# A retention and FP4-linear block on one core: v projected token-major, four heads at once, from group two on

## The reference

```python
xn = layernorm(x)
# retention, 16 heads of 64, on xn
q = heads((xn @ Wq + bq) * 64**-0.5); k = heads(xn @ Wk + bk); v = heads(xn @ Wv + bv)
ret = einsum('bhid,bhjd->bhij', q, k) * D        # D[i,j] = exp(decay_h * (i-j)) where i >= j, else 0
ret = ret / clip(abs(ret.sum(-1)), 1, None)
g = groupnorm_per_head(einsum('bhij,bhjd->bhid', ret, v)) * gn_w + gn_b
attn = (silu(xn @ Wg + bg) * g) @ Wo + bo
# linear layer whose input xn and weight are rounded to 4-bit values with block scales
lin = fp4(xn) @ fp4(weight).T * scale + bias
out = x + attn + lin
```

## Time and profile before

| | us |
|---|---|
| median of 3 runs | 2141.93 |
| lowest, highest | 2136.59, 2142.75 |
| the profiled execution | 2142.48 |
| its span, first to last instruction | 2140.7 |

### The profile page before, as it was taken

The page is one execution under the profiler, slowest core; times in us unless marked ns, Lnnn a source line. Parts: engine busy times, 40 slices in busy tenths (PEclk is TensorE's granted clock), DMA queues, the critical chain, the costliest instruction groups (busy, mean ns, idle before and its releaser), DMA issues.

```text
span 2140.7 us, 51098 instructions
## 1 busy us (share of the span) xinstructions
PE 2080.3 (97%) x18098; PEld 1053.5 (49%) x18098; DVE 1541.7 (72%) x4375; ACT 685.9 (32%) x1318; POOL 640.0 (30%) x456
## 2 busy tenths in 40 slices
PE   5988899999999999999999999999999999999999
PEld 3444444455455454555555555454555454555444
DVE  7899898988889877566767556767656767656732
ACT  5756623332223233322323322323322322322300
POOL 1323232332233333223332223233223233223220
PEclk8999999999999999999999999999999999999999
DMA  8878634334343443323333323333323333223343
GB/s 317 282 253 265 218 98 138 108 109 136 100 127 108 137 128 94 102 83 109 124 103 93 103 84 109 122 103 94 103 85 107 122 103 95 103 86 106 122 153 117
DMA packets 181686, 275.61 MB, mean 129 GB/s; under 512 B 117344, under 2 KB 117472, under 8 KB 181344
## 3 DMA queue, kind: packets, MB, share of 16 engines
q1 hardware_dynamic: 181600, 274.48, 39.8%
HBM read 204.18 MB, written 40.89 MB: 114 GB/s over the span
## 4 chain that ended last, share of the span: by engine, by line
PE 86%; DVE 11%; DMA 2%; issue 1%; ACT 0%; SPq 0%; DVEq 0%; ACTq 0%
PE mm L1288 54%; PE mm L1223 10%; PE tp L1223 6%; PE mm L1232 4%; PE tp L1298 3%; PE four L1338 3%; PE four L1351 2%; PE tp L1326 1%; PE four L1311 1%; PE four L1232 1%; PE tp L1251 1%; DVE wo L929 1%; DMA res<-in_w_f 1%; DMA parts<-wo 1%; DVE state L1041 1%
## 5 line engine op out<-in xcount | busy, mean ns | idle before, releaser
L1288 PE MATMUL mm<-xnT,wring 128*128 128x512 f16 x6144 | 1365.8, 381 | 13.8 <-DVE wring L929 6.8
L1288 PEld LDWEIGHTS mm<-xnT,wring 128*128 128x128 f16 x6144 | 598.2, 98 | 710.3 <-issue 25.2
L695 ACT ACTIVATE work<-four,gs 128x64 f32<-128x64 f32 x512 | 158.1, 414 | 554.2 <-DVE gs L1068 554.2
L556 POOL TENSOR_TENSOR yT<-gn,gate 128x512 f32 (+1 forms) x64 | 84.2, 1315 | 800.6 <-ACT gn L706 800.6
L1223 PE MATMUL mm<-wo,yT 128*128 128x512 f16 x960 | 214.1, 380 | 0.1
L1055 DVE BATCH_NORM_STATS2 gst<-four 128x6 f32<-128x64 f32 x512 | 73.5, 216 | 195.0 <-PE four L1351 194.8
L539 POOL TENSOR_TENSOR qparts<-qT,qparts 128x512 f16<-128x512 f32 x64 | 77.0, 1203 | 363.2 <-ACT qT L664 363.1
L539 POOL TENSOR_TENSOR kparts<-kT,kparts 128x512 f16<-128x512 f32 x64 | 84.2, 1316 | 225.1 <-ACT kT L664 225.1
L1223 PEld LDWEIGHTS mm<-wo,yT 128*128 (+1 forms) x960 | 91.0, 98 | 108.3 <-issue 0.2
L1223 PE MATMUL tp<-wo,yT 128*128 128x512 f16 x576 | 128.2, 379 | 0.0
L662 ACT ACTIVATE qparts<-mm,consts,down 128x512 f16<-128x512 f32 x64 | 49.7, 776 | 213.2 <-PE mm L1288 213.2
(11 more groups left out here) (198 smaller groups left out, 2648.8 us busy)
## 6 DMA issues: line engine op xcount, KB each, us to landing
wring<-parts SPq DMA_DIRECT2D x252, 512.0 KB, 3.9
xt<-in_x SPq DMA_DIRECT2D x34, 512.0 KB, 3.6
out<-res SPq DMA_DIRECT2D x32, 512.0 KB, 3.0
parts<-wo SPq DMA_DIRECT2D x28, 512.0 KB, 5.6
res<-in_x SPq DMA_DIRECT2D x28, 512.0 KB, 3.5
ftile<-in_w_f SPq DMA_DIRECT2D x12, 512.0 KB, 4.4
parts<-wring SPq DMA_DIRECT2D x8, 512.0 KB, 6.8
probs<-in_x SPq DMA_DIRECT2D x5, 512.0 KB, 4.6
```

The source lines that it names most:

```text
L556: nc.gpsimd.tensor_tensor(hi, gn[:], gate[:, u], ALU.mult)
L695: last = nc.scalar.activation(work[:, c * P + h * HD:c * P + (h + 1) * HD], ao[h][:, c * VW:c * VW + HD], ACT.Identity, bias=gs[:, 1, g:g ...
L1288: last = MM(mm[n % 2][:], wring[:, n, wj, k, :], xnT[:, parity, xj, k, :], start=(j == 0), stop=(j == 3 * KT - 1))
```

## The change

From group two on v is projected token-major: the stationary operand is a tile of xnT (128 tokens), the moving one the weights of both pairs, 2 x 128 = 256 columns, taken from the ring's slots 1 and 3 together. One call of `project_v(j)` makes 256 tokens for four heads in 48 matmuls, in two halves of the bank mm1; two calls make the group. The transposes of v are gone. ACT reads each half of v from the bank, scaled, straight into v1, which now holds four heads; POOL adds the bias in place from a table in SBUF (`bias_v`), since it now varies along the columns. state_increments waits for both additions (`v_ready`).

The order on PE becomes: k0, V(0), transpose_g(1), q0, transpose of k0, V(1), k1, scores(0), g0, state_increments(0), attend_within(0), transpose of k1, q1, attend_earlier(0), g1, scores(1), and on as before. On mm1 the uses are V(0), V(1), g0, g1. Slots 1 and 3 hold v of both pairs until V(1) is done, then g of both pairs (`load_gates`), then, after g0 and g1, v of the next body's pairs (`load_v`). In SECOND and THIRD the move of the f tile comes after the last of these loads. `parts` gets one more place, a copy of v of pair 1, made in the second body of the first group, where the bias table of v is loaded too. The first group computes as before; vT now lies on the memory of xqf. Numbers of bank uses and of semaphore rises follow.

```diff
-        vT = sb("vT", [P, GROUP])
+        v_bias = sb("v_bias", [P, E])
-        v1 = sb("v1", [P, CH, 2, VW])
+        v1 = sb("v1", [P, CH, 4, VW])
...
+                def load_gates():
+
+                    w("mm1_full", 2)
+                    for u in range(2):
+                        load_ring(2 * u + 1, 3, q * 2 + u)
+
+                def load_v(u):
+
+                    w("mm1_full", g_use(phase, u))
+                    load_ring(2 * u + 1, 1, q * 2 + 2 + u)
...
+                    if i == 1:
+                        sp.wait_ge(stored[5], 16)
+                        sp.dma_start(a["parts"][1, PAIRS + 1], a["parts"][1, 1]).then_inc(wrap_stored, 16)
+                        sp.dma_start(v_bias[:], a["bv"]).then_inc(v_bias_in, 16)
...
-                for n in range(4):
-                    load_slice(0, n)
+                load_slice(0, 0)
+                load_slice(0, 2)
+                load_gates()
                 move_x_parts()
                 w("xq_ready", 1)
                 load_x(1)
-                for n in range(4):
-                    load_slice(1, n)
+                load_slice(1, 0)
+                load_v(0)
+                load_slice(1, 2)
+                load_v(1)
...
+                def bias_v(j):
+
+                    w("mm1_free", j + 1)
+                    pool.sem_inc(pool_turn, 1)
+                    out = v1[:, 2 * j:2 * j + 2, :, 0:HD]
+                    rows = v_bias[:, ds(q * (2 * P), 2 * P)].rearrange("p (h d) -> p h d", d=HD)
+                    nc.gpsimd.tensor_tensor(out, out, rows.unsqueeze(1).broadcast_to([P, 2, 4, HD]), ALU.add)\
+                      .then_inc(s["v_ready"], 1)
...
                 split(1, kT[:], kparts)
+                if phase != FIRST:
+                    bias_v(0)
                 split(2, qT[:, 0], qparts)
                 decay_q(0)
                 x_lo()
+                if phase != FIRST:
+                    bias_v(1)
                 split(3, kT[:], kparts)
...
+                def evacuate_v(j):
+
+                    w("within", 0)
+                    w("mm1_full", j + 1)
+                    act.sem_inc(act_turn, 1)
+                    for u in range(2):
+                        from_u = mm[1][:].rearrange("p (c a h d) -> p c a h d", c=2, a=2, d=HD)[:, :, u]
+                        last = nc.scalar.activation(v1[:, 2 * j:2 * j + 2, 2 * u:2 * u + 2, 0:HD], from_u,
+                                                    ACT.Copy, scale=down[:, 1, pair(u)])
+                    last.then_inc(s["mm1_free"], 1)
...
                 evacuate(0, 0)
-                evacuate(0, 1)
+                evacuate_v(0)
                 affine(1, 1)
                 x_hi()
                 evacuate(0, 2)
-                copy_v(0)
                 decay_k(0)
+                evacuate_v(1)
+                evacuate(1, 0)
                 evacuate(0, 3)
-                evacuate(1, 0)
-                evacuate(1, 1)
                 decay_k(1)
                 evacuate(1, 2)
-                copy_v(1)
                 normalize(0)
...
+                def project_v(j):
+
+                    if j == 0:
+                        w("w_v", 0)
+                        w("w_g", 0)
+                    w("mm1_free", j)
+                    out = mm[1][:].rearrange("p (c a x) -> p c a x", c=2, a=2)
+                    for c in range(2):
+                        tokens = slice((2 * j + c) * P, (2 * j + c + 1) * P)
+                        n = 0
+                        for k in range(KT):
+                            for wj, xj in ((0, 0), (1, 0), (0, 1)):
+                                last = MM(out[:, c], xnT[:, parity, xj, k, tokens], wring[:, 1::2, wj, k, :],
+                                          start=(n == 0), stop=(n == 3 * KT - 1))
+                                n += 1
+                    last.then_inc(s["mm1_full"], 1)
```

More of the change, by code:

```diff
@@ L120, in bank_uses, with g_use @@
 def bank_uses(phase):
[L122 to L123 removed]
+    if phase == FIRST:
+        t0, t1 = ("k0", "u0", "v1", "u1", "g1"), ("v0", "k1", "g0")
+    else:
+        t0, t1 = ("k0", "u0", "u1", "g1"), ("k1", "g0")
     return {n: (0, i + 1) for i, n in enumerate(t0)} | {n: (1, i + 1) for i, n in enumerate(t1)}
+def g_use(phase, u):
+    return mm_use(u, 3) if phase == FIRST else 3 + u
 def mm_use(u, n):
@@ L399, in store_late, with load_ring @@
                     sp.dma_start(a["out"][ds(j * GROUP + i * P, P), :], late_bufs[j][:]).then_inc(late_out[j], 16)
+                def load_ring(n, matrix, pair):
+                    src = a["parts"][matrix, ds(pair, 1)].rearrange("a p n -> p (a n)")
+                    sp.dma_start(wring[:, n].rearrange("p a b c -> p (a b c)"), src)\
+                      .then_inc(s["w_" + MATS[n]], 16)
+                def load_gates():
[5 more added lines that the diff above has]
+                    load_ring(2 * u + 1, 1, q * 2 + 2 + u)
                 if phase == TAIL:
@@ L1277, in project @@
                 def project(u, n):
-                    use = mm_use(u, n)
+                    use = g_use(phase, u) if n == 3 else mm_use(u, n)
+                    slot = n
+                    if n == 3 and phase != FIRST:
+                        slot = 2 * u + 1
                     if (phase, i, u) == (FIRST, 0, 0):
@@ L1282, in project @@
                     else:
-                        w("w_" + MATS[n], u)
+                        w("w_" + MATS[slot], u if slot == n else 1)
                     w(f"mm{n % 2}_free", use - 1)
@@ L1287, in project @@
                         for wj, xj in ((0, 0), (0, 1), (1, 0)):
-                            last = MM(mm[n % 2][:], wring[:, n, wj, k, :], xnT[:, parity, xj, k, :],
+                            last = MM(mm[n % 2][:], wring[:, slot, wj, k, :], xnT[:, parity, xj, k, :],
                                       start=(j == 0), stop=(j == 3 * KT - 1))
@@ L1313, in scores, with v_head @@
                     last.then_inc(s["scores_full"], 1)
+                def v_head(u, h):
+                    return h if phase == FIRST else 2 * u + h
                 def state_increments(u):
                     bk, use = uses[f"u{u}"]
-                    for which in "kv":
+                    for which in ("kv" if phase == FIRST else "k"):
                         b, n = uses[f"{which}{u}"]
                         w(f"t{b}_free", n)
+                    if phase != FIRST:
+                        w("v_ready", 2)
                     w(f"t{bk}_free", use - 1)
@@ L1325, in state_increments @@
                         for h in range(2):
-                            last = MM(increment(bk, k)[h * HD:(h + 1) * HD], kn[rows, c, h, :], v1[rows, c, h, :],
+                            last = MM(increment(bk, k)[h * HD:(h + 1) * HD], kn[rows, c, h, :], v1[rows, c, v_head(u, h), :],
                                       start=True, stop=True)
@@ L1360, in body @@
                     sum_slices(0, 4, 4)
-                project(0, 1)
+                if phase == FIRST:
+                    project(0, 1)
+                else:
+                    project_v(0)
                 if phase != FIRST or i:
@@ L1364, in body @@
                 project(0, 2)
-                transpose_kv(0, "v", vT, 1)
+                if phase == FIRST:
+                    transpose_kv(0, "v", vT, 1)
                 transpose_kv(0, "k", kT, 0)
-                project(0, 3)
+                if phase == FIRST:
+                    project(0, 3)
+                else:
+                    project_v(1)
                 project(1, 0)
@@ L1375, in body @@
                     sum_slices(i + 1, 0, SLICES)
-                project(1, 1)
+                if phase == FIRST:
+                    project(1, 1)
+                else:
+                    project(0, 3)
                 if phase == FIRST and i == 0:
```

51 lines of the change are left out of this document (30 added, 21 removed), and 4 rows, old and new, of the table PER.

## The result

| | median (range), us | runs | profiled run, its span, us |
|---|---|---|---|
| before | 2142.19 (2136.59 to 2142.75) | 4 | 2142.48, 2140.7 |
| after | 2157.09 (2156.03 to 2158.43) | 4 | 2158.43, 2156.6 |

The ratio is 1.0076, with a 95% interval of 1.0058 to 1.0094: the changed kernel is slower by 0.8%, where I had forecast 0.5% faster. The prediction was wrong, in its range and in its sign.

What follows compares the result with a forecast made beforehand. PE's instruction list was taken to bound 27 of the 28 changed bodies. From 2142.48 us, -15.0 + 1.4 + 1.5 + 1.0 = -11.1 gave 2131.4, predicted as 2131 us, range 2120 to 2145.

Steps and rivals of the forecast that it cites:

- PE's list: Changed bodies on PE: transposes gone -0.87 us, 96 matmuls at 109.2 ns +0.12, net -0.75 us per body.
- The rival that a 256-column matmul doesn't hide its load: v's projections on PE: 205 ns per load and matmul, +9.2 us per body, 2380 us; chance 0.04.
- the Trainium skill's rule: PE weight loads overlap running matmuls only where row groups differ; 205 ns a pair, kernel some 2400 us.
- ACT and the weights: ACT's evacuations and g's later weight loads: no cost; bounds about 1 us a body each if cover failed or loads were late.
- GpSimd's additions and DVE's air: Long loop: two additions delay DVE's mask 1.2 to 2.3 us against 2.6 us left; holds, barely.
- rival (b): Long loop: split(3) and the biases' addition catch the last quantizing operation; about 2164 us; chance 0.10, half-way forms 0.08.
- Groups two and three: Zero slack at transpose_g(0), group_norm enters late: -0.3 to +0.4 us a body, taken +0.2, for 7 bodies +1.4.
- The first body of group two: PE already waits 2.58 us for DVE's mask, DVE comes later still: -0.3 to +2.5 us, taken +1.5.
- Start, first group, tail: Start and first group: doubled ones memset +0.5 us, extra queue traffic +0.5, together +1.0.
- -15.0: Long loop: 20 bodies gain 0.75 us each, in all -15.0 us, if DVE's mask stays in time.

Runs made afterwards that it cites:

- e2: Kernel after, with GpSimd's output-bias addition moved behind decay_q(1) in the long loop, waiting for group_norm's statistics; 2132.73 us, ratio 0.9974.
- e1: Kernel after without GpSimd's two additions of v's bias, which is left out of the computation; 2118.66 us, ratio 0.9912.
- e3: Kernel after, with GpSimd's output-bias addition moved behind decay_q(1) in groups two and three as well as the long loop; 2130.57 us, ratio 0.9966.
- e7: Kernel after, with ACT writing v's scaled bias into the PSUM bank before each half instead of GpSimd's additions; 2242.53 us, ratio 1.0484.
- e9: Kernel after, with GpSimd adding only the first half's bias and ACT writing the second half's into PSUM before its matmuls; 2125.94 us, ratio 0.9928.
- e5: Kernel before, v still by transposes, plus two GpSimd additions on spare memory in the places of the two new ones; 2165.32 us, ratio 1.0131.

## Why the prediction was wrong, step by step

- **PE's list: right.** 109.2 ns from start to start as forecast; a body without a wait takes 63.30 us where 64.1 was before (forecast -0.75). The rival that a 256-column matmul doesn't hide its load fell with the row at 905.14, and with it the Trainium skill's rule (TensorE: Matmul & The Clock Gate, The mechanism) for these full-height loads. In e2 the loop's 19 intervals gave 15.3 us.
- **ACT and the weights: right.** No wait of PE for wring or for v's evacuation in the list of waits, and e1, which keeps both, loses nothing.
- **GpSimd's additions and DVE's air: the step that failed.** The air was about right: 2.6 us forecast, 2.8 by the latest start of 4.9, the 1.8 at which the mask mostly stood before and the 0.3 by which PE comes earlier. The delay was forecast at 1.2 to 2.3 us. It was 2.2 to 2.7 in eight bodies (from 1.3 to 1.8 us before to 4.2 or 4.3 after the scores, less the same 0.3), which held, and 4.1 to 4.8 in twelve, which didn't; against the same bodies of e1 it is 2.5 to 2.6 and 4.3 to 5.0. "After each POOL operation one DVE operation gets through" is true and was my argument against rival (b); but I had applied it to the wrong operation. The one that gets through behind split(3) is the one that split(3) held. I took that to be the last, L842. L841 ended where L842 starts, 1304.19, so with its length of 0.69 and the hand-over it starts 0.72 before, at 1303.47. State_increments is 5.79 behind the scores' start, so the scores start at 1308.78 - 5.79 = 1302.99, and L841 0.48 behind them; 0.3 for PE's earlier arrival and my own 1.2 to 1.7 us of delay make it 2.0 to 2.5, and split(3) starts at 2.3: my own range had both kinds of body in it. I had put 0.59 on the one and 0.18 on the other. The first kind's L903 stands at 2.11 and the second's at 2.72. The step that was never worked out is which operations stand on either side of split(3) over the whole range of the delay.
- **Rival (b) is what happened**, in 12 of 20 bodies. Its mechanism was named (the last quantizing operation held by the biases' addition), its price was 1.6 us a body, and 1.9 was measured. One thing differs: (b) had a single operation held by split(3) and the biases' addition in turn; what ran was two operations, one held by each. It was priced at 2164 for all 20; with twelve the kernel lands at 2157.
- **A cost I had not listed: the clock.** In two bodies of the loop the wait was followed by a drop. The busy times of three stretches (the wait's, the drop's, the next) in the kernel after; the granted clock is the last number but two:

```profile
1116.00:1125.00 9.00, 6.81 (x83) 3.08 (x84) 8.46 (x11) 2.22 (x3) 4.38 (x2) 1.00 0.41 65
1125.70:1129.00 3.30, 3.30 (x35) 2.57 (x31) 2.13 (x8) 0.65 (x2) 0.00 (x0) 0.50 0.88 324
1130.00:1140.00 10.00, 10.00 (x106) 4.66 (x108) 5.10 (x23) 1.45 (x2) 2.42 (x2) 1.00 0.16 58
```

  PE stood still for 2.2 of the 9 us, then ran at 0.50, the lower of its two levels (1.2 GHz), and was back at 2.4 GHz behind it. Those bodies take 67.1 and 66.9 us, where 63.3 and their waits of 2.19 and 1.92 make 65.5 and 65.2: some 1.7 us each, +3.4 with what rounding leaves. The other ten waits had no drop.
- **Groups two and three: the mechanism right, the size wrong.** Forecast: waits of 0.4 to 1 us at transpose_g(0), +0.2 a body, at worst +0.8; measured: seven waits of 1.3 to 1.6, +0.9 a body without the first, so +1.4 became +6.0. First the f tile's last operation in the kernel before, ahead of group_norm, then body 7 of the kernel after, DVE and POOL, answering to the earlier trace rows:

```profile
497.39 0.69 DVE L842 TENSOR_TENSOR xqf<-xa,qs 128x512 bf16<-128x512 f32 x1
```

```profile
501.78 1.67 DVE L903 TENSOR_TENSOR xa<-xa,xm 128x512 f32<-128x512 f32 x1
503.48 1.64 DVE L904 TENSOR_TENSOR xqf<-xa,qs 128x512 bf16<-128x512 f32 x1
505.31 1.15 DVE L1117 BATCH_NORM_STATS2 gst<-four 128x6 f32<-128x64 f32 x8 [0.19 <-DVE xqf L904]
```

```profile
501.74 1.15 POOL L577 TENSOR_TENSOR qparts<-qT,qparts 128x512 f16<-128x512 f32 x1 [11.28 <-ACT qT L717]
503.09 1.48 POOL L584 TENSOR_TENSOR qT<-qT,qfac 128x512 f32<-128x512 f32 x1 [0.20 <-POOL qparts L577]
504.53 2.79 POOL L609 TENSOR_TENSOR res<-res,out_bias 128x1024 f32<-128x1024 f32 x1
```

  group_norm can't start before the f tile is quantized, and the delayed tile's last two operations, which had come ahead of split(4) (at 499.32 before), now stand under split(4) and the decay and take 1.67 and 1.64 instead of 0.69. So group_norm starts 4.6 us after the PE work that it reads has ended (at 500.67), and 0.1 before. I had counted a late entry of under 2.3 us less its air, and the five short operations behind the biases' addition, 0.7 us, but not two long ones moved under GpSimd ahead of it. e1 shows the part that would be kept: 60.8 us a body, -0.4, where I had said -0.3.
- **The first body of group two: right.** +1.4 us measured, +1.5 forecast.
- **Start, first group, tail: small, as forecast, but -2.4 against +1.0**, and that by luck. The scores of body 0 come at 65.14 us instead of 64.16, +1.0. Body 3 is 1.5 us shorter (58.66 against 60.16, at a mean granted clock of 0.97 against 0.91), and the tail, which holds a part of body 31's own gain, 1.6 (0.99 against 0.97). Drops of the clock there fall differently from kernel to kernel, so no part is put to the change.

Put together by the sum's own terms: -15.0 was -15.3 and then +26.3, +1.4 was +6.0, +1.5 was +1.4, +1.0 was -2.4. The loop's waits and their clock are the error; without them the sum would have been on the right side, as e2 shows, which takes the loop's waits away and lands at 0.9974 of the kernel before, 2133 us beside 2138.

## What to carry to other kernels

When work is added to GpSimd, don't add up the time it takes from VectorE: lay out both queues, shift VectorE's by the smallest and by the largest delay, and see which VectorE operation each following GpSimd operation then catches; a shift past one GpSimd start costs the length of the next GpSimd operation at once. Ask of each wait that an edit removes, or each instruction that it adds to an idle engine, what stands ahead of it in that engine's order and what is due next behind it (e3, e7). An addition to a matmul's result can cost nothing that shows if it is written into the bank before the matmuls and the writing engine has a projection's time ahead of its turn (e9: its loop bodies take 63.3 us as in e1, and it is 0.7% faster than the kernel before); where it hasn't, it cost over 100 us (e7).

## What the runs showed of the hardware that I had not expected

- The same two GpSimd additions make VectorE 2.2 to 2.7 or 4.1 to 4.8 us later, with nothing between, and in bodies 14 and 23 a difference of 0.03 us in the order of two starts (L886 and L594) stands at the head of the one and the other.
- A held operation ends 0.55 us after the GpSimd operation's end (931.32 and 930.77; 1253.45 and 1252.90; 1256.20 and 1255.65), close to the 0.69 that it takes alone. So it seems to wait for the GpSimd operation's whole length and then run; this is inferred.
- Operations of VectorE that read PSUM pass under GpSimd unhindered also here (L1087 starts at 931.24 inside L609 and takes its 0.74 for two); a scalar_tensor_tensor with both inputs in SBUF doesn't (L886: 0.23 or 1.35).
- GpSimd may be slower for it too: the biases' addition took 2.79 and 2.80 us in these two bodies, in which a held operation or the mask stands under it, and 2.35 in the kernel before, where the mask had ended ahead of it. No run isolates this.
- PE waits of about 2 us were followed by a stretch at a granted clock of 0.50 in 2 of 12 cases in the kernel after and in none of the nine in e5 (1.8 to 2.1 us). In e7, with 26 waits of 2.9 us on average (76.4 us), such a stretch lies at 20 of them. What decides isn't told by these runs.
